# A decoder layer in fp32 on one core: the projection of cross attention three key blocks later

## The chip, the core and the metric

The kernel runs on one core of a Trainium2 chip. The metric is the device time of one execution in microseconds (us). TensorE (PE) does the matmuls, VectorE (DVE), ScalarE (ACT) and GpSimd (POOL) the rest, SyncE (SP) issues the transfers. Each engine works through its own queue in order and waits on semaphores.

## What is computed

A decoder layer on x of 2048 tokens by 256: causal self attention with 16 heads of 16, cross attention with 16 heads of 64 to a context of 1601 rows, then a small feed-forward product in fp8 values. What matters here is the cross attention:

```python
q = (query @ Wq + bq).reshape(b, sq, N_HEAD, KEY_DIM)
k = (key @ Wk + bk).reshape(b, key.shape[1], N_HEAD, KEY_DIM)
v = (value @ Wv + bv).reshape(b, value.shape[1], N_HEAD, VALUE_DIM)
scores = jnp.einsum('bqhd,bkhd->bhqk', q, k) / TEMP
attn = jax.nn.softmax(scores, axis=-1)
out = jnp.einsum('bhqk,bkhd->bqhd', attn, v).reshape(b, sq, N_HEAD * VALUE_DIM)
out = out @ Wo + bo + residual
```

## The kernel before

All work is laid out in one list of stages, which the class `Order` makes. Each engine's program walks through the same list and issues what it has to do for each stage, so a stage's place in the list sets its place in every queue.

Cross attention goes through 8 pairs of heads (`NP`, p = 0 to 7), and in each pair through 4 blocks of 512 queries (`NB`, b = 0 to 3). A block of queries meets 13 key blocks of up to 128 rows (`NS`, j = 0 to 12):

- `pair_scores` (TensorE L904, L912): scores of one key block into one of four PSUM buffers for each head; ScalarE takes the exponentials (L1079) into a ring of 11 weights buffers. GpSimd adds the exponentials up over the key blocks (L698, one addition for each head and key block from j = 1 on), for the softmax's divisor. In the last pair VectorE adds for one of the two heads.
- `pair_values` (L924): products with the values, summed over the key blocks in PSUM.
- `pair_finish` (ScalarE L1093): the products are copied to one of two buffers `o_pair`. The next block's products for j = 0 wait for that copy.
- `pair_sums` (TensorE L935, ScalarE L976): the sums over the rows of the added exponentials, copied to `pair_recip`.
- `pair_invert` (VectorE L1283): four reciprocals of 128 columns.
- `pair_divide` (GpSimd L1434): `o_pair` times the reciprocals.
- `pair_project` (TensorE L947): the projection with the output weights: four tiles of queries, into two of the three PSUM banks that the side work also uses. VectorE adds each bank to the residual (L1292). After the fourth block of a pair, SP loads the output weights of the pair after the next (L1457).

The score steps run in groups of two key blocks. After each group, `pair_values` of `Order` counts as many steps as key blocks are pending, and puts in the stages that have come due; only then it puts in the products of the group before. `after(n, ...)` makes a stage come due n steps on. With `SUMS_LAG` the sums follow the finish by 4 steps. From the sums, the reciprocals follow by 1 to 4 steps, the division by 5 and the projection by `PROJECT_LAG` = 8, so by 12 from the finish. As a block has 13 steps, the projection of a block stands after the scores of key block 12 of the next block, and ahead of the next block's products of 10 and 11.

Into this main work the side work is spread: the first sweep of the next pair (`pair_chunk`: scores for the maxima, TensorE L889, VectorE L1189; `pair_negate` and `pair_rows` for the shifts), and the next but one pair's projections of keys (L723, then ScalarE L1055 and L1064, VectorE L1252, GpSimd L1422) and queries (ScalarE L1058, VectorE L1239) and the value tiles (L877). This side work shares the three banks in turn. The projections of keys stand around the beginning of each pair. The last pair has no side work of this kind; its projections are followed by the tail of the layer (`tail`).

Of the kernel before, what the change touches and what calls it, by code (L numbers as in the profile page):

```python
# [21 lines left out]
NB, TB = T // BQ, BQ // P  # L22
# [3 lines left out]
FOLD_LAG, TURN_LAG, OUT_LAG = 2, 2, 2  # L26


SUMS_LAG, PROJECT_LAG = 4, TB + 4

SELF_RING, SELF_SCORES = 4, 3
CROSS_RING, NSCORES = 3, 4
# [9 lines left out]
NP = H // HP  # L42
# [76 lines left out]
class Order:  # L119
# [104 lines left out]
    def pair_sums(self, p, b):  # L224
        self.put("pair_sums", p, b, banks=1)
        for t in range(TB):
            self.after(t + 1, lambda t=t: self.put("pair_invert", p, b, t))
        self.after(TB + 1, lambda: self.put("pair_divide", p, b))
        self.after(PROJECT_LAG, lambda: self.pair_out(p, b))

    def pair_sweep2(self, p):
        batch = []
# [1402 lines left out]
```

## Time and profile before

| | us |
|---|---|
| median of 3 runs | 2157.15 |
| lowest, highest | 2141.8, 2167.85 |
| the profiled execution's own time | 2139.68 |
| its span, first to last instruction | 2137.7 |

The profile records one execution. PE is the matmul part of TensorE, PEld its weight loads. An instruction is named by its engine and by its line in the kernel (L947); each fp32 matmul of the kernel shows up as more than one record. PEclk is the clock that TensorE was granted as a share of 2.4 GHz; its two levels are 1.2 and 2.4 GHz. Cross attention lasts from about 727 us to the end, the last pair's own part from about 1956 us. The share of busy time of an engine over the span mixes stages, so the rows below are cut by stage. A row of waits names the engine and line that stood idle, and whose end came last before it went on.

### The profile page before, as it was taken

What the parts mean: (1) busy time and instruction counts of PE and PEld (TensorE: products, weight loads), DVE (VectorE), ACT (ScalarE), POOL (GpSimd) and SP (SyncE); (2) the same over time, 40 slices, a digit from 0 to 9 for tenths busy, and PEclk for the clock granted to TensorE, in tenths of its full rate; (3) what the DMA queues carried; (4) which work ended last, traced back from release to release, by engine and by line L of the source; (5) the groups of instructions that cost most, each with busy time, mean ns of one, the idle gap of its engine ahead of it and who ended that gap; (6) DMA issues with size and microseconds to landing.
All of it is one profiled execution on the core that took longest, in us unless ns stands there. A gap on an engine that the chain in (4) does not pass through costs nothing.

```text
span 2137.7 us, 29456 instructions
## 1 busy us (share of the span) xinstructions
PE 1862.8 (87%) x10650; PEld 949.8 (44%) x10650; DVE 1295.8 (61%) x2455; ACT 916.6 (43%) x1866; POOL 1036.1 (48%) x872
## 2 busy tenths in 40 slices
PE   6888999889998998898999899889889889989671
PEld 3544444434444544444445445445445445444331
DVE  4677766766712557746636545645654653667888
ACT  2235655555644343244343343344344434434331
POOL 1000000000000466558777777877876886886664
PEclk9669999998967899999999899999999999999875
DMA  5222201240011000000000000000000000000001
GB/s 106 29 33 32 32 8 25 32 88 1 1 30 40 19 1 1 1 10 12 1 1 12 1 1 12 1 1 12 2 1 3 1 1 3 1 10 21 0 21 39
DMA packets 28745, 34.46 MB, mean 16 GB/s; under 512 B 4099, under 2 KB 26948, under 8 KB 26948
## 3 DMA queue, kind: packets, MB, share of 16 engines
q1 hardware_dynamic: 28600, 32.59, 8.5%
q8 instruction: 85, 1.39, 0.3%
q14 instruction: 60, 0.48, 0.1%
HBM read 14.99 MB, written 4.19 MB: 9 GB/s over the span
## 4 chain that ended last, share of the span: by engine, by line
PE 47%; issue 26%; POOL 10%; DVE 8%; ACT 6%; SPq 2%; DMA 1%; POOLq 0%; ACTq 0%; DVEq 0%
PE psum L924 8%; POOL parts_room L698 7%; PE psum L809 7%; PE psum L904 6%; PE psum L784 5%; PE psum L757 4%; PE psum L947 4%; ACT weights_room L1007 3%; PE psum L889 3%; DVE maxima L1189 3%; PE psum L723 2%; POOL parts_room L1434 2%; PE psum L821 2%; ACT weights_room L1079 1%; PE psum L793 1%
## 5 line engine op out<-in xcount | busy, mean ns | idle before, releaser
L1189 DVE TENSOR_REDUCE maxima<-psum 128x1 f32<-128x400 f32 (+5 forms) x1664 | 864.1, 579 | 351.5 <-PE psum L889 192.4
L698 POOL TENSOR_TENSOR parts_room<-parts_room,weights_room 128x512 f32<-128x512 f32 (+1 forms) x606 | 761.2, 1284 | 133.1 <-ACT weights_room L1079 128.1
L1079 ACT ACTIVATE weights_room<-psum 128x512 f32<-128x512 f32 (+1 forms) x757 | 402.2, 601 | 568.8 <-PE psum L904 387.3
L1007 ACT ACTIVATE weights_room<-psum 128x512 f32<-128x512 f32 (+3 forms) x640 | 297.8, 535 | 248.2 <-PE psum L784 133.8
L1396 POOL TENSOR_SCALAR rstd<-meanvar 128x2 f32<-128x2 f32 (+1 forms) x24 | 8.0, 333 | 708.6 <-DVE meanvar L1139 708.6
L904 PE MATMUL psum<-stack_room,dk_hi 64*128 64x512 f32 (+1 forms) x1408 | 269.4, 410 | 18.7 <-ACT weights_room L1079 18.7
L889 PE MATMUL psum<-k_later,stack_room 64*128 64x400 f32 (+1 forms) x896 | 245.5, 404 | 33.1 <-DVE maxima L1189 32.0
L784 PE MATMUL psum<-stack_room,stack_room 51*128 51x512 f32 (+3 forms) x640 | 201.6, 452 | 45.9 <-ACT weights_room L1007 44.5
L889 PEld LDWEIGHTS psum<-k_later,stack_room 64*128 64x128 f32 x896 | 129.5, 184 | 205.3 <-issue 103.2
L924 PE MATMUL psum<-weights_room,parts_room 128*64 128x512 f32 (+1 forms) x754 | 211.5, 627 | 0.0
L924 PE MATMUL psum<-weights_room,late_room 128*64 128x512 f32 (+1 forms) x760 | 208.9, 622 | 0.0
L757 PE MATMUL psum<-stack_room,stack_room 51*128 51x512 f32 (+3 forms) x640 | 166.0, 480 | 19.5 <-DVE maxima L1189 13.5
L809 PE MATMUL psum<-weights_room,v_self 128*32 128x512 f32 (+3 forms) x1280 | 178.7, 614 | 0.0
L904 PEld LDWEIGHTS psum<-stack_room,dk_hi 64*128 64x128 f32 (+1 forms) x1408 | 148.9, 182 | 57.4 <-ACT weights_room L1079 31.4
L904 PE MATMUL psum<-stack_room,dk_lo 64*128 64x512 f32 (+1 forms) x704 | 173.9, 393 | 0.0
L947 PE MATMUL psum<-parts_room,parts_room 128*128 128x256 f32 x256 | 98.9, 553 | 72.9 <-POOL parts_room L1434 72.9
L784 PEld LDWEIGHTS psum<-stack_room,stack_room 51*128 51x128 f32 x640 | 97.2, 204 | 130.6 <-ACT weights_room L1007 107.9
L698 POOL TENSOR_TENSOR parts_room<-weights_room,weights_room 128x512 f32<-128x512 f32 x49 | 61.8, 1276 | 184.7 <-ACT weights_room L1079 184.7
L757 PEld LDWEIGHTS psum<-stack_room,stack_room 51*128 51x128 f32 x640 | 72.9, 206 | 141.1 <-issue 115.8
L1292 DVE TENSOR_TENSOR stack_room<-psum,stack_room 128x512 f32<-128x512 f32 x64 | 43.8, 690 | 128.9 <-PE psum L947 128.5
L1283 DVE RECIPROCAL parts_room<-parts_room 128x128 f32<-128x128 f32 x128 | 112.5, 918 | 0.0
L947 PEld LDWEIGHTS psum<-parts_room,parts_room 128*128 128x128 f32 x256 | 67.3, 275 | 96.9 <-POOL parts_room L1434 84.3
(133 smaller groups left out, 1987.5 us busy)
## 6 DMA issues: line engine op xcount, KB each, us to landing
stack_room<-parts_room SPq DMA_DIRECT2D x96, 128.0 KB
x_block<-x_dram SPq DMA_DIRECT2D x8, 512.0 KB, 4.8
x_middle<-x_block SPq DMA_DIRECT2D x4, 512.0 KB, 3.1
x_block<-x_middle SPq DMA_DIRECT2D x4, 512.0 KB, 3.9
out_dram<-x_block SPq DMA_DIRECT2D x8, 256.0 KB, 2.1
parts_room<-ctx_dram SPq DMA_DIRECT2D x1, 1536.0 KB
stack_room<-shift_rows SPq DMA_DIRECT2D x64, 2.0 KB
parts_room<-wq_dram SPq DMA_DIRECT2D x8, 128.0 KB, 2.2
```

What stands on the lines that cost most here:

```text
L698: engine.tensor_tensor(sum_[:kw, :], old[:kw, :], weights[u % NP_WEIGHTS][:kw, :], ALU.add) \
L757: last = engine.matmul(slots[m][:, 0:k1 - k0], q_stack[p % NSTACK][r, i * P:(i + 1) * P], k_stack[p % NSTACK][r, k0:k1], start=True, stop= ...
L784: last = engine.matmul(self_scores[u % SELF_SCORES][:, 0:n], k_stack[p % NSTACK][r, j * P:(j + 1) * P], q_stack[p % NSTACK][r, q0:q0 + n], ...
L809: last = engine.matmul(products[c:c + COL, q0:BQ], v_self[:, j0 + n, h * VW:h * VW + COL], w_self[(s0 + n) % NW][:, m, 0:BQ - q0], start=j ...
L889: filled(use + n, engine.matmul(slot[:, 0:k1 - k0], q_hi[p % 2][r:r + DH2, i * P:(i + 1) * P], k_high(p)[r:r + DH2, k0:k1], start=True, st ...
L904: last = engine.matmul(pair_scores[u % NSCORES][:kw, :], k[r:r + DH2, at:at + kw], q[r:r + DH2, block(b)], start=first and n == 0, stop=no ...
L924: engine.matmul(products[r:r + DH2, :], v_pair[p % 2][:kw, j, r:r + DH2], weights[u % NP_WEIGHTS][:kw, :], start=j == 0, stop=j == NS - 1) \
L947: last = engine.matmul(slot[:, t * D:(t + 1) * D], o_pair[n_block % 2][:, i * P:(i + 1) * P], wo2[p % 2], start=True, stop=True)
L1007: engine.activation(w_self[s % NW][:, m, 0:n], self_scores[(HP * s + m) % SELF_SCORES][:, 0:n], ACT.Exp, scale=SELF_SCALE).then_inc(exp_do ...
L1079: engine.activation(weights[u % NP_WEIGHTS][:kw, :], pair_scores[u % NSCORES][:kw, :], ACT.Exp, scale=CROSS_SCALE).then_inc(pair_exp, 1)
L1189: engine.tensor_reduce(maxima[:, p % 2, i // TB, n, i % TB, ch:ch + 1], bank_of(use + n)[:, 0:real - k0], AX.X, ALU.max) \
L1283: engine.reciprocal(pair_recip[:, cols], pair_recip[:, cols]).then_inc(inverted, 1)
```

## The change

The projection's lag counts 11 steps from the sums in place of 8, which is 15 from the finish, except in the last pair, where it stays at 8. Nothing else in the kernel differs.

```diff
-SUMS_LAG, PROJECT_LAG = 4, TB + 4
+SUMS_LAG, PROJECT_LAG, LAST_PROJECT_LAG = 4, TB + 7, TB + 4
...
         self.after(TB + 1, lambda: self.put("pair_divide", p, b))
-        self.after(PROJECT_LAG, lambda: self.pair_out(p, b))
+        self.after(PROJECT_LAG if p < NP - 1 else LAST_PROJECT_LAG, lambda: self.pair_out(p, b))
```

`TB` is 4. `pair_out` puts in the stage `pair_project`, the load of output weights after a fourth block, and in the last pair the tail.

## Rows read from the trace of the kernel before

**Rows 1.** The page's first part: busy time of each engine and its share of the span.

```profile
span 2137.7 us, 29456 instructions
...
PE 1862.8 (87%) x10650; PEld 949.8 (44%) x10650; DVE 1295.8 (61%) x2455; ACT 916.6 (43%) x1866; POOL 1036.1 (48%) x872
```

**Rows 2.** Table of stretches by projection: length, busy per engine (count), PEclk, DMA share, GB/s.

```profile
827.03:979.75 152.72, 139.94 (x721) 73.29 (x721) 95.49 (x181) 54.11 (x106) 96.19 (x80) 0.99 0.03 7
979.75:1142.51 162.76, 147.63 (x800) 77.42 (x800) 91.36 (x169) 68.16 (x133) 126.78 (x105) 0.98 0.02 5
1142.51:1313.16 170.65, 155.45 (x801) 81.15 (x801) 91.34 (x169) 68.18 (x133) 126.80 (x105) 0.92 0.02 4
1313.16:1481.08 167.92, 152.74 (x801) 80.37 (x801) 91.36 (x169) 68.17 (x133) 126.75 (x105) 0.94 0.02 5
1481.08:1643.97 162.89, 147.67 (x800) 77.07 (x801) 91.34 (x169) 68.17 (x133) 126.88 (x105) 0.98 0.01 2
1643.97:1808.31 164.34, 149.15 (x801) 78.74 (x801) 91.36 (x169) 68.17 (x133) 126.85 (x105) 0.97 0.01 2
1808.31:1955.68 147.37, 133.16 (x702) 68.03 (x702) 96.46 (x163) 60.41 (x117) 112.61 (x90) 0.91 0.04 12
```

**Rows 3.** Waits of cross attention, 727 to 1956 us: engine, line, releaser: total, times, longest.

```profile
POOL parts_room L698 <- ACT weights_room L1079: 281.5, 88, 25.3
...
DVE stack_room L1292 <- PE psum L947: 128.5, 50, 7.5
...
PE psum L947 <- POOL parts_room L1434: 70.7, 28, 3.8
...
PE psum L889 <- DVE maxima L1189: 36.3, 69, 0.8
```

**Rows 4.** Timeline of one stall, 1168 to 1186 us: start, duration, engine, line, work, idle before.

```profile
1172.46 2.20 ACT L1079 ACTIVATE weights_room<-psum 128x512 f32<-128x512 f32 x4 [2.25 <-PE psum L904]
...
1173.46 6.17 POOL L698 TENSOR_TENSOR parts_room<-parts_room,weights_room 128x512 f32<-128x512 f32 x5
...
1176.53 0.40 PE L904 MATMUL psum<-stack_room,dk_lo 64*65 64x512 f32 x2
...
1179.60 1.25 POOL L1434 TENSOR_TENSOR parts_room<-parts_room,parts_room 128x512 f32<-128x512 f32 x1
...
1180.91 3.78 PE L947 MATMUL psum<-parts_room,parts_room 128*128 128x256 f32 x8 [3.58 <-POOL parts_room L1434]
1183.02 0.69 DVE L1292 TENSOR_TENSOR stack_room<-psum,stack_room 128x512 f32<-128x512 f32 x1 [4.75 <-PE psum L947]
```

**Rows 5.** TensorE's timeline at five projections, between 975 and 1225 us.

```profile
979.75 1.99 PE L947 MATMUL psum<-parts_room,parts_room 128*128 128x256 f32 x8 [1.84 <-POOL parts_room L1434]
...
1015.22 3.62 PE L947 MATMUL psum<-parts_room,parts_room 128*128 128x256 f32 x8 [3.55 <-POOL parts_room L1434]
...
1054.28 1.99 PE L947 MATMUL psum<-parts_room,parts_room 128*128 128x256 f32 x8 [1.58 <-POOL parts_room L1434]
...
1089.58 2.90 PE L947 MATMUL psum<-parts_room,parts_room 128*128 128x256 f32 x8 [3.76 <-POOL parts_room L1434]
...
1220.85 3.78 PE L947 MATMUL psum<-parts_room,parts_room 128*128 128x256 f32 x8 [1.58 <-POOL parts_room L1434]
```

**Rows 6.** TensorE's timeline from a projection to the second pair of next products, 1952 to 1970 us.

```profile
1955.68 2.00 PE L947 MATMUL psum<-parts_room,parts_room 128*128 128x256 f32 x8 [2.18 <-POOL parts_room L1434]
1957.61 1.94 PE L924 MATMUL psum<-weights_room,late_room 128*64 128x512 f32 x8
...
1962.52 0.73 PE L904 MATMUL psum<-stack_room,dk_hi 64*128 64x512 f32 x4
...
1964.11 1.94 PE L924 MATMUL psum<-weights_room,late_room 128*64 128x512 f32 x8
```

**Rows 7.** Timeline around key projections, 1095 to 1125 us, where the third block's projection will stand.

```profile
1102.01 2.38 PE L723 MATMUL psum<-parts_room,parts_room 128*128 128x512 f32 x8
...
1105.33 1.00 DVE L1252 SCALAR_TENSOR_TENSOR parts_room<-psum,parts_room,parts_room 128x512 f32<-128x512 f32 x2 [2.28 <-ACT k_later L1055]
...
1105.90 1.98 PE L723 MATMUL psum<-norm_room,parts_room 128*128 128x512 f32 x4
...
1109.75 0.75 DVE L1239 SCALAR_TENSOR_TENSOR stack_room<-psum,parts_room,stack_room 128x512 fp32r<-128x512 f32 x1 [3.42 <-ACT stack_room L1058]
```

**Rows 8.** One line of the source, the reciprocals on VectorE, whole span: its head.

```profile
L1283 DVE RECIPROCAL parts_room<-parts_room x128: 887/937/947, 809.4 to 2098.4; 128x128 f32<-128x128 f32 x128
```

## The prediction

> **What bounds the kernel now.** I read the page's first part, then the stretches, then the waits, then a stall in its timeline. TensorE is busy for 87% of the span, the next engine for 61% [rows 1]. The change touches cross attention's first seven pairs, so the stretches are cut from one projection of a block to the same one a pair later [rows 2]: 162.76 to 170.65 us a whole pair (the last row is a shorter one), TensorE busy for 147.6 to 155.5 of it, GpSimd 126.8, VectorE 91.4, ScalarE 68.2. TensorE is the bound, and lacks some 15.2 us of being busy throughout in each pair.
>
> The waits say what most of that is [rows 3]. From 727 to 1956 us TensorE stood before the projection (L947) for GpSimd's division (L1434) 70.7 us in 28 waits: once for each of the four blocks of the seven pairs. Its wait for VectorE's maxima is next, 36.3 us in 69 pieces of at most 0.8. VectorE stood 128.5 us for the projection, since its addition (L1292) comes next in its queue; that is the same stall seen behind TensorE, not a second cost.
>
> The timeline shows why the division is late [rows 4]. It comes in GpSimd's queue behind the additions of key blocks 10 and 11. ScalarE makes their exponentials from 1172.46 to 1174.66, GpSimd does five additions in 6.17 us (1.234 each), then the division at 1179.60, to 1180.85. TensorE began the last matmuls of key block 12 at 1176.53 and was through 0.8 us later; it starts the projection at 1180.91. In a steady pair the four stalls are 1.8, 3.6, 1.6 and 3.8 us [rows 5].
>
> A second cost comes with them. Eight matmuls of the projection take 1.99 us at 979.75 and at 1054.28, and 3.78 us at 1180.91 and 1220.85 [rows 4, 5]. The granted clock falls from 2.4 to 1.2 GHz at the stalls: the pair with PEclk 0.98 lasts 162.89 us, the one with 0.92 170.65 [rows 2], with the same instructions.
>
> **The change part by part.** No instruction is added or removed; one step moves. It goes three key blocks later. Counted on TensorE's queue it passes the products of key blocks 10 and 11, the scores of key blocks 0 and 1 of the next block, the products of key block 12, the scores of 2 and 3, and the pieces of side work that lie between. It lands right ahead of the products of 0 and 1. The sums, the reciprocals and the division stay where they are. On ScalarE it has no instruction; on VectorE its two additions move past the maxima or key steps in between. GpSimd's queue doesn't have it. On SP, the load of the output weights (L1457, six times) moves with it; no transfer of shifts lies between the old place and the new, and these weights are wanted two pairs later. Buffers hold: the sums of two blocks alternate, and the eviction that needs the projected buffer again comes 26 key blocks after the first, against 15 for the projection.
>
> *Stall.* What TensorE has to do between the old place and the new is from the end of a projection to the second group of eight products. It is shortest where there is no side work: 1957.68 to 1964.11, 6.4 us [rows 6]; with side work it is more. The stall ahead of it is 2.2 us there, and no stall is over 3.8 [rows 3, 6]. So even the shortest way after the longest stall leaves the division ready with 2.6 us in hand, and the 70.7 us go. I take all of it; the lower bound is what follows if GpSimd falls further behind, below.
>
> *GpSimd's pace*, since it loses the pause that TensorE's stalls gave it. A block costs it 24 additions of 1.234 and a division of 1.25, 30.9 us [rows 4]. TensorE's shortest interval is from 979.75 to 1015.22, 35.47 us, less its stall of 3.55: 31.9; the third is 1089.58 - 1054.28 = 35.30, less 3.76: 31.5 [rows 5]. The other two of the pair are 39.06 and 52.93. GpSimd has 0.6 us to spare in the tight ones and 5 or more in the others. It keeps up, and does not build a queue from block to block.
>
> *Clock.* The share of a pair at 1.2 GHz is twice what PEclk lacks: 27.3 us of 170.65 and 6.5 of 162.89. The pairs differ by 7.76 us for 20.8 us more at the lower level: 0.37 us lost for each us. Less than a half, since part of such a stretch is the stall itself. Over the seven rows [rows 2] the time at the lower level is 3.1 + 6.5 + 27.3 + 20.2 + 6.5 + 9.9 + 26.5 = 100 us, times 0.37 is 37 us. The bounds are nothing (it falls anyway) and 50 us (one half of 100). I take 37, since every slow group of the projections' rows follows a wait, and TensorE has hardly any idle time left when these waits are gone.
>
> *The new place.* Two of three banks are taken at once there. In the third block of a pair it stands behind projections of keys, whose banks VectorE frees late. There the four blocks of keys are projected by 1104.4, VectorE's last key step ends at 1106.3, and TensorE finishes the first query projection at 1107.9 [rows 7]; so the banks are free when the projection comes. Behind it the next query projection needs a bank that is read at 1110.5, while TensorE has the projection (2.0) and products (1.9) to do first: nothing to wait for. I take 0; the bound is the 3.42 us that VectorE waited there for ScalarE, in one block of four: seven times 3.42, 24 us.
>
> *Sum.* 70.7 + 37 = 108 us off the profiled execution: span 2137.7 - 108 = 2030; its own time was 2139.68, 2.0 above its span, so 2032. The median of the runs, 2157.15, is 17.5 us above that execution. If this comes from more time at the lower clock at the stalls, the change takes it away too, and I take 2032 for the median; if it sits elsewhere, the time is near 2049.
>
> **The rivals.**
> 1. *GpSimd paces.* There is no addition for key block 0, so GpSimd may stand for one key block in each short block (31.7 / 13 = 2.4 us), which makes its block 33.3 where TensorE's is 31.7: 1.6 us in 14 blocks, 22 us, with half of the clock's gain lost, 18. Time 2072. For it: 30.9 against 31.5 is close. Against: GpSimd waited for ScalarE 281.5 us in cross attention [rows 3], so it has room, and a delay of its division is harmless until it passes the slack above.
> 2. *The clock stays as it is.* Only the stalls go: 2139.7 - 70.7 = 2069. For it: 36.3 us of short waits on maxima stay [rows 3]. Against: 979.75 and 1054.28 have stalls of 1.8 and 1.6 with no slow matmul, and between the stalls the rows show full speed. The Trainium skill, TensorE: Matmul & The Clock Gate, in the section on psum-queue depth-cycling, describes a kernel whose matmul groups run through PSUM banks with so many small idle moments that the clock oscillates. By it this ring of three banks would keep it oscillating, and the sum would be without its clock term; this trace has 0.99 in the first stretch, where VectorE reads banks most densely (181 instructions in 152.7 us against 169 in 162.8 [rows 2]).
> 3. *The gain is given back at once*: the stalls only absorb another engine's lateness, and TensorE waits as long at the next maxima or scores. 2140 to 2157. For it: VectorE and GpSimd work on or catch up meanwhile. Against: outside of the stalls TensorE is busy nearly all the time, and no engine is busy for more than 126.8 of the 148 us that a pair would take.
> 4. *Slower.* VectorE is late at the new place: the bank ring of three is held by its queue, four reciprocals of 0.918 [rows 8] and two additions of 0.69 [rows 4], 5.1 us, and TensorE waits for a bank behind each of 28 projections, its clock as low as now. That adds 143 us where 71 are saved: 2140 + 72 = 2212. It takes the whole gain of the stalls from 71 / 28 = 2.5 us a block, and is slower by over 1% of the median (2179) from (71 + 39) / 28 = 3.9. Against: the reciprocals are due three to six key blocks after the new place, and had been done long before the old one; VectorE is busy for 91 us of 165.
>
> **How the numbers follow.** The forecast (2010 to 2055) has 62%, rival 1 12%, rival 2 10%, rival 3 8%, rival 4 5%; 3% for a time under 2010. Predicted 2032. The low end is 2032 less the 13 us of the clock's upper bound and some lateness of the maxima that goes too, 2010; the high end takes in rivals 1 and 2 and the 24 us of bank waits beside part of the median's distance: 2085. A measurement of this kernel can tell about 1% from no change. Faster by over 1%: 62 + 12 + 10 + 3 = 87%. Within 1%: 8%. Slower: 5%.
>
> **What would show it.** In the profile after, no wait of L947 on L1434 in pairs 0 to 6 (the one of the last pair's first block stays, about 2.2 us). Pairs of 148 to 151 us between like projections, with TensorE busy for all but some 4 us, and eight projection matmuls in 1.99 us. PEclk 0.98 or more from 830 us to the last pair. GpSimd's busy time per pair stays 126.8. The last pair stays as long as it is. I would be wrong if L947 waited for a bank, if L1434 still ended after the place reached, if ScalarE waited for L698, or if TensorE showed 1.2 GHz in the middle of a block with no idle time before it.

## The result: 5.7% faster, and the stages that gave it

The changed kernel takes 2025.67 us in the median of 4 runs (2021.61 to 2040.59) against 2149.48 us before (2138.02 to 2167.85). The ratio is 0.943, with an interval of 0.934 to 0.952. The profiled execution has a span of 2026.2 us where the kernel before has 2137.7, 111.5 us less. The prediction had 2030 for the span and 2032 for the time. A ratio, here and below, compares only those executions that lie within 1.5% of the fastest of the same kernel, so it is not always the quotient of the medians.

The page after differs in few places: TensorE is busy 1815.9 us (90%) in place of 1862.8 (87%), with the same 10650 matmuls; VectorE (1297.4) and GpSimd (1041.1) do what they did. First the table of stretches of the kernel after; columns as in [rows 2]. The first row ends where the first scores of cross attention begin, the second at the sums (L935) of the first pair's fourth block. The three rows in the middle run from the fourth block's projection of a pair to that of the next. The last two are cut at the sums of fourth blocks again.

```profile
0.00:732.00 732.00, 640.84 (x4269) 318.48 (x4269) 435.03 (x899) 363.23 (x787) 26.92 (x40) 0.87 0.21 34
732.00:949.80 217.80, 204.56 (x1004) 105.59 (x1004) 141.10 (x274) 83.43 (x163) 138.60 (x115) 0.97 0.02 5
981.72:1130.62 148.90, 143.89 (x801) 75.80 (x801) 91.07 (x170) 68.23 (x135) 127.16 (x105) 1.00 0.02 5
1130.62:1279.52 148.90, 143.86 (x800) 75.89 (x801) 91.08 (x170) 68.21 (x135) 127.22 (x105) 1.00 0.02 5
1577.43:1726.39 148.96, 143.95 (x800) 76.01 (x801) 91.07 (x170) 68.21 (x135) 127.21 (x105) 1.00 0.01 2
1694.50:1830.20 135.70, 130.66 (x771) 70.34 (x770) 95.56 (x168) 59.69 (x116) 119.81 (x96) 1.00 0.04 13
1830.20:1973.80 143.60, 110.35 (x570) 51.47 (x568) 124.25 (x177) 60.12 (x117) 97.33 (x77) 0.87 0.02 8
```

And four stretches of the kernel before, with the cuts of the first two and the last two of these:

```profile
0.00:735.00 735.00, 644.35 (x4269) 319.67 (x4269) 435.39 (x899) 362.78 (x787) 26.88 (x40) 0.87 0.21 34
735.00:954.00 219.00, 202.80 (x1004) 102.49 (x1003) 141.03 (x274) 83.14 (x163) 138.33 (x115) 0.99 0.02 5
1782.60:1939.50 156.90, 141.73 (x769) 75.68 (x768) 95.44 (x174) 59.71 (x116) 118.90 (x96) 0.91 0.03 9
1939.50:2085.40 145.90, 111.18 (x570) 51.48 (x568) 121.10 (x171) 60.09 (x118) 95.54 (x77) 0.87 0.03 10
```

What the reader is to see: a whole pair lasts 148.9 to 149.0 us, every one, where [rows 2] had 162.8 to 170.7. TensorE is busy for 143.9 of that, so it lacks 5.0 us where it lacked 15.2; PEclk is 1.00 where it went down to 0.92. Up to the first scores the two differ by 3 us (735.0 against 732.0), which is no effect of the change, as its queues are the same there. So cross attention gave 108.5 of the 111.5 us: 1402.7 from first scores to the end before, 1294.2 after. The last pair, whose own order is as it was, takes 198.2 us before (145.9 and the 52.3 behind it) and 196.0 after (143.6 and 52.4); the difference is about the stall of the pair before it, 2.2 us, that fell into it.

The waits of cross attention after, from 727 to 1900 us, which takes in the first 50 us of the last pair's own part (columns as in [rows 3]):

```profile
POOL parts_room L698 <- ACT weights_room L1079: 194.3, 102, 26.1
...
PE psum L889 <- DVE maxima L1189: 37.1, 71, 0.8
...
DVE stack_room L1292 <- PE psum L947: 11.6, 37, 0.7
...
PE psum L947 <- POOL parts_room L1434: 2.5, 1, 2.5
```

The 28 waits for the division are gone. The one that is left, of 2.5 us, is the last pair's own first block; its like before (2.2 us) lies behind the window of [rows 3]. VectorE's wait for the projection went with them, 128.5 to 11.6 us. The maxima are as they were (36.3 before, 37.1 after): nothing was handed on to the next wait. GpSimd stands for the exponentials for 194 us where it stood for 281 [rows 3]: it has less idle time, as the same work stands in a shorter span.

The timeline at the same projection as in [rows 4], block 0 of the third pair, after the change:

```profile
1156.34 1.34 POOL L1434 TENSOR_TENSOR parts_room<-parts_room,parts_room 128x512 f32<-128x512 f32 x1
...
1162.40 0.52 PE L889 MATMUL psum<-k_later,stack_room 64*128 64x402 f32 x2
...
1162.85 1.99 PE L947 MATMUL psum<-parts_room,parts_room 128*128 128x256 f32 x8
1164.02 0.69 DVE L1292 TENSOR_TENSOR stack_room<-psum,stack_room 128x512 f32<-128x512 f32 x1 [0.15 <-PE psum L947]
```

The division ends at 1157.68, the projection begins at 1162.85, without idle time ahead of it and at full speed, 1.99 us for the eight matmuls. Here the division is 5.2 us ahead; in the other blocks of a steady pair 7.2, 10.8 and 6.3.

### The profile page after: what moved, and what is told of

Its sections match the earlier page's. It is cut to its first block, busy times and chain, and to the rows that moved or that the text cites. A ratio compares the mean times of both kernels' runs of the same rounds, so it can differ in the third digit from the quotient of the medians.

```text
span 2026.2 us, 29464 instructions
## 1 busy us (share of the span) xinstructions
PE 1815.9 (90%) x10650; PEld 931.0 (46%) x10650; DVE 1297.4 (64%) x2455; ACT 917.6 (45%) x1866; POOL 1041.1 (51%) x872
## 4 chain that ended last, share of the span: by engine, by line
PE 74%; DVE 15%; ACT 5%; issue 2%; SPq 2%; DMA 1%; POOL 1%; ACTq 0%; POOLq 0%; DVEq 0%
PE psum L924 16%; PE psum L904 14%; PE psum L889 8%; PE psum L809 7%; DVE maxima L1189 7%; PE psum L723 6%; PE psum L784 5%; PE psum L757 4%; ACT weights_room L1007 4%; PE psum L947 3%; PE psum L877 3%; DVE parts_room L1283 2%; PE psum L821 2%; PE psum L935 1%; DVE parts_room L698 1%
## 5 line engine op out<-in xcount | busy, mean ns | idle before, releaser
L698 POOL TENSOR_TENSOR parts_room<-parts_room,weights_room 128x512 f32<-128x512 f32 (+1 forms) x606 | 764.6, 1293 | 164.0 <-ACT weights_room L1079 158.3
L924 PE MATMUL psum<-weights_room,late_room 128*64 128x512 f32 (+1 forms) x760 | 204.4, 609 | 0.0
L924 PE MATMUL psum<-weights_room,parts_room 128*64 128x512 f32 (+1 forms) x754 | 202.7, 605 | 0.0
L757 PE MATMUL psum<-stack_room,stack_room 51*128 51x512 f32 (+3 forms) x640 | 165.6, 480 | 19.7 <-DVE maxima L1189 13.6
L904 PEld LDWEIGHTS psum<-stack_room,dk_lo 64*128 64x128 f32 (+1 forms) x704 | 98.4, 183 | 10.1
L924 PEld LDWEIGHTS psum<-weights_room,late_room 128*64 128x64 f32 (+1 forms) x760 | 51.4, 138 | 86.3 <-issue 83.3
L698 POOL TENSOR_TENSOR parts_room<-weights_room,weights_room 128x512 f32<-128x512 f32 x49 | 63.5, 1312 | 52.3 <-ACT weights_room L1079 52.3
L924 PEld LDWEIGHTS psum<-weights_room,parts_room 128*64 128x64 f32 (+1 forms) x754 | 50.8, 136 | 82.2 <-issue 78.8
```

The costliest lines, as they stand in the source:

```text
L698: engine.tensor_tensor(sum_[:kw, :], old[:kw, :], weights[u % NP_WEIGHTS][:kw, :], ALU.add) \
L757: last = engine.matmul(slots[m][:, 0:k1 - k0], q_stack[p % NSTACK][r, i * P:(i + 1) * P], k_stack[p % NSTACK][r, k0:k1], start=True, stop= ...
L904: last = engine.matmul(pair_scores[u % NSCORES][:kw, :], k[r:r + DH2, at:at + kw], q[r:r + DH2, block(b)], start=first and n == 0, stop=no ...
L924: engine.matmul(products[r:r + DH2, :], v_pair[p % 2][:kw, j, r:r + DH2], weights[u % NP_WEIGHTS][:kw, :], start=j == 0, stop=j == NS - 1) \
```

## Experiments

All are compared with the kernel before on the same chip. As the part of the program ahead of cross attention, which none of them touches, takes 722.0 to 736.2 us in their traces, a pair's length in the trace says more than the time. What the stretches show is one execution of each kernel.

### The clock's share alone

The stall is kept and filled: TensorE multiplies into the bank that the projection will overwrite.

```diff
+FILL = (6, 2, 6, 3)
...
-                pe.wait_ge(divided, n_block + 1)
                 pe.wait_ge(wo_pair_in[p % 2], 16 * (p // 2 + 1))
+                slot = take_bank(use)
+                for _ in range(FILL[b] if p < NP - 1 else 0):
+                    engine.matmul(slot[:, 0:D], ident[:, :], wo2[p % 2], start=True, stop=True)
+                pe.wait_ge(divided, n_block + 1)
```

> The kernel before, with matmuls that nobody reads put ahead of the projection's wait for the division in pairs 0 to 6: 6, 2, 6 and 3 of them (128x256, about 0.5 us each at full speed) for blocks 0 to 3, written to the bank that the projection overwrites. TensorE works instead of standing, so the stalls' time stays and only the clock may change. If 37 us of the gain are the clock's, as predicted: about 2140 - 37 = 2103 (ratio to before 0.98), PEclk 0.98 or more in the steady pairs, and pairs of some 160 us. If the clock fell for another reason, or its fall cost nothing: no change, 2140 and PEclk of 0.92 to 0.98 as before. If the clock were most of the gain: near 2050.

Measured: 2100.02 us (2094.08 to 2137.18), ratio 0.974 (0.968 to 0.981). A pair of its table of stretches, and its timeline at the third pair's block 0. In this kernel L945 is the filling, L951 the projection and L1438 the division:

```profile
1109.70:1269.30 159.60, 152.60 (x837) 81.96 (x836) 91.39 (x169) 68.17 (x133) 126.92 (x105) 1.00 0.02 5
...
1167.43 2.83 PE L945 MATMUL psum<-parts_room,ident 128*128 128x256 f32 x12
1169.59 1.25 POOL L1438 TENSOR_TENSOR parts_room<-parts_room,parts_room 128x512 f32<-128x512 f32 x1
...
1170.90 1.78 PE L951 MATMUL psum<-parts_room,parts_room 128*128 128x256 f32 x7 [0.64 <-POOL parts_room L1438]
```

All five steady pairs are 159.5 or 159.6 us. The projection still waits for the division, 0.64 us behind the filling that ends at 1170.26, but now takes its full speed. So the same order with the same lateness, without the fall of the clock, is 159.6, and 148.9 without the stalls: 10.7 us a pair are the stalls, which is the 10.8 read in [rows 4, 5]. What the clock cost is the rest: 3 us in the pairs that had 0.98, 11 us in the one with 0.92. From the first pair's last sums to the last pair's last sums (seven stretches), 1131.4 us before became 1089.7 here and 1024.0 in the changed kernel: 41.7 for the clock, 65.7 for the stalls. The expectation had 37 and some 2103 us.

### The cause: the division's place in GpSimd's queue

The projection stays at its old place; the division comes one step earlier, ahead of the additions of key blocks 10 and 11.

```diff
-        self.after(TB + 1, lambda: self.put("pair_divide", p, b))
+        self.after(TB, lambda: self.put("pair_divide", p, b))
```

> The kernel before, with the projection where it was and the division one step earlier, so that it stands ahead of the additions of key blocks 10 and 11 in GpSimd's queue. If the cause is that the division was behind four additions, no stall of L947 on L1434 is left and the gain is the whole of the change's: about 2030, ratio 0.945. If the later place of the projection itself brought something (the banks, the queue of VectorE), less than that: the stalls go, but pairs stay above 149 us. If GpSimd now stands for VectorE's reciprocals and falls behind with its additions, a part comes back as a wait for L1434 or L698: 2060 to 2100.

Measured: 2036.86 us (2025.81 to 2042.83), ratio 0.945 (0.939 to 0.951). Two of its stretches, a steady pair and the one before the last sums, and its timeline at two projections:

```profile
1095.70:1244.60 148.90, 144.25 (x801) 75.83 (x800) 91.41 (x169) 68.16 (x133) 126.88 (x105) 1.00 0.02 5
1827.90:1977.70 149.80, 110.95 (x571) 51.85 (x570) 125.43 (x173) 60.05 (x117) 94.17 (x76) 0.86 0.03 11
...
1148.78 1.27 POOL L1434 TENSOR_TENSOR parts_room<-parts_room,parts_room 128x512 f32<-128x512 f32 x1
...
1150.01 3.74 POOL L698 TENSOR_TENSOR parts_room<-parts_room,weights_room 128x512 f32<-128x512 f32 x3
...
1151.58 1.75 PE L947 MATMUL psum<-parts_room,parts_room 128*128 128x256 f32 x7
...
1843.22 1.76 DVE L1283 RECIPROCAL parts_room<-parts_room 128x128 f32<-128x128 f32 x2
...
1845.12 1.51 POOL L1434 TENSOR_TENSOR parts_room<-parts_room,parts_room 128x512 f32<-128x512 f32 x1 [6.18 <-DVE parts_room L1283]
...
1846.69 1.65 PE L947 MATMUL psum<-parts_room,parts_room 128*128 128x256 f32 x3 [4.85 <-POOL parts_room L1434]
```

The pair is 148.9 us, the same as with the change, though only GpSimd's queue was touched. So the stall was the division's lateness behind four additions; the later place of the projection brings nothing beyond that. The division ends 1.5 us ahead of the projection here. But where VectorE adds too, in the last pair, the same order stalls by 4.85 us: there the division at the head waits for VectorE's reciprocals (1843.22 to 1844.98), and the stretch is 149.8 us against 143.6 with the later projection. The two ways are alike in the steady pairs. At the end the later projection is some 6 us shorter in these two traces, which the times (0.945 and 0.943, with intervals that overlap) can't tell.

### Half of the blocks

The change for blocks 0 and 2 alone.

```diff
-        self.after(PROJECT_LAG if p < NP - 1 else LAST_PROJECT_LAG, lambda: self.pair_out(p, b))
+        self.after(PROJECT_LAG if p < NP - 1 and b in (0, 2) else LAST_PROJECT_LAG, lambda: self.pair_out(p, b))
```

> The change for blocks 0 and 2 only, where the stalls were 3.6 and 3.8 us in a steady pair; blocks 1 and 3, with 1.6 and 1.8, keep the old place. Stalls of 46 us go and 24.4 stay. If short stalls do not bring the clock down by themselves, the whole clock term (37) goes too: 2140 - 46 - 37 = 2057, ratio 0.961, and eight projection matmuls take 1.99 us in all blocks. If each stall brings it down on its own, half of that term: 2076, ratio 0.97, with 3.8 us projections in blocks 1 and 3.

Measured: 2065.05 us (2054.7 to 2077.38), ratio 0.959 (0.952 to 0.967). Two neighbouring pairs, and the projections of blocks 1 and 3 in the third pair:

```profile
948.60:1103.60 155.00, 147.15 (x803) 77.72 (x802) 91.11 (x169) 68.17 (x133) 126.87 (x105) 0.98 0.02 5
1103.60:1255.50 151.90, 144.05 (x801) 75.89 (x800) 91.12 (x169) 68.19 (x133) 126.91 (x105) 1.00 0.02 5
...
1198.57 1.78 PE L947 MATMUL psum<-parts_room,parts_room 128*128 128x256 f32 x7 [1.58 <-POOL parts_room L1434]
...
1281.23 2.07 PE L947 MATMUL psum<-parts_room,parts_room 128*128 128x256 f32 x4 [1.86 <-POOL parts_room L1434]
```

The pairs go 155.0, 151.9, 155.1, 151.9, 153.6. With 148.9 + 1.6 + 1.8 = 152.3 for a pair with its two short stalls and a full clock, 151.9 is that, and 155 is that with slow matmuls. In the rows, a stall of 1.58 us is followed by fast matmuls, one of 1.86 by slow ones (2.07 us for the four that the line holds). Over the six pairs from 950 us on, both outcomes occur for both lengths (1.58: slow in 2 of 6, 1.86: slow in 4 of 6), and the granted clock is 1.00 in the 3 us ahead of each. So a short stall alone can bring the clock down, but not each time. The seven stretches take 1061.1 us: 1024.0, 22.8 of stalls, and 14.3 more. Of these, 2.5 us are a wait of TensorE for ScalarE's exponentials at 1851.92, which neither the kernel before nor the changed one has; the rest, under 12 us, is mainly the clock, against its 41.7 before. The ratio is that of the first expectation, but its mechanism is not quite: it had no slow matmuls left.

### The exception for the last pair

The change without its exception.

```diff
-SUMS_LAG, PROJECT_LAG, LAST_PROJECT_LAG = 4, TB + 7, TB + 4
+SUMS_LAG, PROJECT_LAG, LAST_PROJECT_LAG = 4, TB + 7, TB + 7
```

> The change without its exception: the last pair's projections too come three key blocks later, and the tail of each block, which starts with its projection, with them. Pairs 0 to 6 stay as in the changed kernel (149 us). In the last pair one wait for the division goes (2.5 us), and the tails of blocks 0 to 2 start some 5 us later, where VectorE is the busier engine. If VectorE has no room there, the end comes later by about 5 us: near 2031. If it has, it is the same or 2 us less: 2024 to 2028. If the exception were what made the change good, clearly slower than 2040.

Measured: 2025.51 us (2015.85 to 2038.51), ratio 0.941 (0.934 to 0.948). Its last two stretches:

```profile
1823.40:1959.50 136.10, 107.31 (x564) 48.63 (x562) 120.53 (x168) 59.71 (x116) 95.08 (x74) 0.87 0.03 8
1959.50:2014.00 54.50, 12.00 (x52) 6.34 (x52) 46.58 (x103) 10.49 (x20) 23.55 (x28) 0.53 0.12 39
```

136.1 and 54.5 us where the changed kernel has 143.6 and 52.4: 5.4 us less at the end. But from the first scores to the end it has 2014.0 - 723.1 = 1290.9 us against 1294.2. Both were run once more.

> The changed kernel without its exception once more. In the first run its pair before the end was 136.1 us where the changed kernel has 143.6, and the stretch behind the last sums 54.4 against 52.4: 5.5 us less. If that holds, its ratio to the kernel before is 0.2 to 0.3% lower than that of the changed kernel, near 2021.

> The changed kernel once more, for comparison with its form without the exception on the same chip: near 2026, ratio 0.943.

Measured: 2020.19 us (2014.7 to 2048.64), ratio 0.945 (0.939 to 0.952) without the exception, and 2021.28 us (2014.31 to 2028.87), ratio 0.945 (0.940 to 0.950) with it. From first scores to the end it is 1289.6 without and 1290.3 with. The times show no difference: 0.2 to 0.3% is less than they can tell. The sums from the first scores on don't tell either, as they hold the first pair's stretch, which varies by 4 us (215.2 to 219.6) with falls of the clock. The stretches behind it do show one. The last two stretches with the exception are 143.6 + 52.4 = 196.0 and, the second time, 142.1 + 52.4 = 194.5; without it 136.1 + 54.5 = 190.6 and 137.0 + 54.1 = 191.1. From the first pair's last sums to the end it is 1076.4 and 1075.1 us with the exception, 1071.3 and 1071.7 without, while the steady pairs are 148.9 to 149.1 in all four traces. So the exception does not make the change; it costs some 3 to 5 us, close to the 5.5 read from the first trace. The wait of 2.5 us for the division is part of it; the rest was not traced.

### How much room GpSimd has

The changed kernel with more multiplications on GpSimd ahead of each division, into a buffer that is not read then; two of them, then four.

```diff
+                for _ in range(2 if at[0] < NP - 1 else 0):
+                    chain.on(engine.tensor_tensor(added[n_block % 2][:, 0, :], o_pair[n_block % 2], pair_recip,
+                                                  ALU.mult))
+                    after_last()
                 engine.tensor_tensor(o_pair[n_block % 2], o_pair[n_block % 2], pair_recip, ALU.mult) \
```

> The changed kernel with two more multiplications on GpSimd ahead of each division in pairs 0 to 6, into a buffer that nobody reads then. That is 2.5 us a block later for the division and everything behind it. In the changed kernel the division is done 5.2, 7.2, 10.8 and 6.3 us ahead of the projection in the blocks of a steady pair, and 2.7 and 0.8 us in the two projections that fall into the last pair. If there is room, only the last one stalls, by some 2 us: pairs of 149 us, time 2026 to 2032 where the changed kernel has 2026. If GpSimd paces already (rival 1), each block pays: 28 times 2.5, near 2095.

Measured: 2030.4 us (2023.87 to 2050.98), ratio 0.951 (0.942 to 0.959). A steady pair:

```profile
1099.00:1248.10 149.10, 144.11 (x803) 76.09 (x802) 91.11 (x169) 68.18 (x133) 137.16 (x113) 1.00 0.02 5
```

GpSimd does 137 us of work in 149, 10 more than before, and the pair's length doesn't move. In block 0 the division still ends 2.1 us ahead of the projection. Only the last moved projection stalls, by 4.7 us rather than the 2 I had expected: there the three multiplications take 5.5 us (1850.50 to 1855.97), where the division alone took 1.5.

> The same with four such multiplications: 4.9 us a block, GpSimd's work 35.8 us where TensorE's shortest interval between projections is 32.2, and 146.5 of 149 us over a pair. If the reserve is what the trace of the changed kernel shows, GpSimd falls behind in the short blocks by more than the 5.2 us: the waits for the division come back, 1 to 4 us in one or two blocks of each pair, and the slow clock with them: 3 to 8 us a pair, time 2050 to 2085. If the reserve is larger: as the changed kernel.

Measured: 2073.07 us (2070.84 to 2092.46), ratio 0.972 (0.962 to 0.981). A steady pair and its timeline at the third pair's block 0, where L1435 is the added work and L1438 the division:

```profile
1105.40:1259.30 153.90, 145.68 (x801) 76.53 (x800) 91.12 (x169) 68.23 (x133) 146.96 (x121) 0.99 0.02 5
...
1166.09 5.34 POOL L1435 TENSOR_TENSOR parts_room<-parts_room,parts_room 128x512 f32<-128x512 f32 x4
...
1171.51 1.26 POOL L1438 TENSOR_TENSOR parts_room<-parts_room,parts_room 128x512 f32<-128x512 f32 x1
...
1172.82 2.60 PE L947 MATMUL psum<-parts_room,parts_room 128*128 128x256 f32 x7 [3.22 <-POOL parts_room L1438]
```

With 147 us of 154 GpSimd now paces in the one place where the interval is shortest: block 0 stalls by 3.2 us in every pair, the matmuls behind it are slow, and the pair is some 5 us longer. The other three blocks have no wait for the division. So rival 1 exists, but only above the load that the kernel has: 127 us a pair is free, 137 still is, 147 isn't.

## Why the prediction was right

**The bound and the stall.** Both held: 70.7 us of waits in 28 pieces went, one of 2.5 us in the last pair stayed (2.2 forecast). The pairs were to be 148 to 151 us and are 148.9. TensorE was to lack some 4 us in each and lacks 5.0.

**The sum.** 108 us forecast; 108.5 in cross attention, 111.5 over the span, the rest being the 3 us before it. Its two terms are now measured apart. The clock's was forecast 37 and is 41.7 over seven stretches. The slope of 0.37 us for a microsecond at the lower level was a little low: by PEclk the first six of these stretches held 99 us at that level before (the seventh takes 145.9 us with the filling too), and 41.7 over 99 is 0.42. The stalls' was 70.7, of which 3.8 lie ahead of those stretches; 66.9 against 65.7 measured. In the stretch with the first pair's stalls (3.8 us) the profiled execution gained only 1.2 (219.0 to 217.8), as its clock fell three times there (0.97, where the kernel before fell once and had 0.99); in the second profile of the changed kernel, with one fall, that stretch is 215.2, which is the 3.8. So the sum hits closer than its terms: a clock term that was 4.7 too low and stalls that gave back 3.8 less (65.7 and 1.2 for 70.7) nearly cancel, and that part of the closeness is luck.

**GpSimd's pace.** I had worked out that it keeps up with 30.9 us of work a block against intervals of 31.5 and more. The intervals after are 32.2, 36.2, 37.8 and 42.7 us, as the projection now stands in other places of the side work, and it does keep up. The 31.5 was taken from the old places and belongs to no interval after. With two multiplications a block costs it 33.4 us, more than the shortest 32.2, and still nothing stalls in the steady pairs; the division's lead in block 0 goes from 5.2 to 2.1. That the limit was near, as rival 1 said, is shown too, with its distance.

**The slack** was the weak step. I said 2.6 us at least between division and projection. In the steady pairs it is 5.2 and more. In the last one that was moved it is 0.8:

```profile
1848.25 1.54 POOL L1434 TENSOR_TENSOR parts_room<-parts_room,parts_room 128x512 f32<-128x512 f32 x1 [3.69 <-DVE parts_room L1283]
...
1850.61 1.99 PE L947 MATMUL psum<-parts_room,parts_room 128*128 128x256 f32 x8
...
1872.50 3.26 PE L947 MATMUL psum<-parts_room,parts_room 128*128 128x256 f32 x8 [2.53 <-POOL parts_room L1434]
```

These are the last moved projection (1850.61) and the first that isn't (1872.50, with its stall). GpSimd had stood 3.69 us for VectorE's reciprocals, which I had counted as ready: in the last pair VectorE also adds exponentials, and they come in its queue among these additions. They were done 13.6 us behind the sums in the kernel before (1939.52 to 1953.08) and 18.0 here (1830.16 to 1848.11). I had read the old stall's length there as GpSimd's lateness alone. It was within the room, and cost nothing; with two multiplications more it was not, and gave the 4.7 us above.

**The new place** cost next to nothing, where I took nothing. L947 does wait for a bank, which I had named as a sign of being wrong: 2.9 us in six pieces, for ScalarE's copy of the shifts, in the second block of a pair. The third block's projection, among the keys, has no wait. Another sign, ScalarE waiting for L698, showed once, for 1.9 us at the beginning of the last pair, behind VectorE's additions. Neither is of a size that bears on the sum.

**Rival 2**, the clock stays, fell: 1.00 in all steady pairs, with the same short waits on maxima. The Trainium skill, TensorE: Matmul & The Clock Gate, on psum-queue depth-cycling, tells of a kernel whose small idle moments between matmul groups keep the clock oscillating. In the steady pairs of this one such moments, of at most 0.8 us, do not; the measurement decides for this kernel. But in the first pair they are all that stands ahead of the clock's three falls. Groups of scores of the same size ahead of one and behind it:

```profile
910.46 0.62 PE L904 MATMUL psum<-stack_room,dk_hi 64*128 64x512 f32 x4
...
914.83 1.40 PE L889 MATMUL psum<-k_later,stack_room 64*128 64x400 f32 x3 [0.67 <-DVE maxima L1189]
...
917.71 1.55 PE L904 MATMUL psum<-stack_room,dk_hi 64*128 64x512 f32 x4
```

The granted clock is 1.00 from 911 to 915 us and 0.73 from 915 to 920; the other two falls follow waits for maxima of 0.47 us (786.80) and 0.48 us (830.77). TensorE waits for maxima 11.0 us in this stretch of 217.8, and 4.3 in a steady pair of 148.9. The two falls more than in the second profile of this kernel go with 2.6 us (217.8 and 215.2). What tells the first pair from the others was not tested. **Rival 3** fell with the waits after, where nothing took the place of the one removed. **Rival 4**, a bank held by VectorE, fell with the 11.6 us that VectorE waits for the projection and with no bank wait of L947 behind VectorE.

**The median.** I took the predicted 2032 for the median rather than 2049, betting that the distance of the median before from its profiled execution came from the clock at the stalls. The median came out at 2025.67, and at 2021.28 in the second series, while the kernel before stayed near 2150. The kernel with the filled stalls points the same way: by the times it gains 2.6%, some 55 us, where the traces have 41.7 for the clock. But its interval, 0.968 to 0.981, is 41 to 70 us, so where those 10 to 17 us lie is not shown, and the bet was not more than that.

## What to carry to other kernels

When the bounding engine waits for a result at the head of its queue, look in the queue of the engine that makes it for what stands ahead: the fix may be on either side, a later consumer or an earlier producer, and both gave the same 149 us a pair. Price the stall with its aftermath: here 65.7 us of waits carried 41.7 us of slow matmuls. Before counting on it, compare the producer's work per block with the consumer's shortest interval after the change, and look at the stages where a third engine has more to do, since the slack goes there first.

## What the runs showed of the hardware

A stall of 1.6 to 1.9 us on TensorE had the matmuls behind it run at 1.2 GHz in some cases and not in others, in one and the same execution. The last pair's stall of 2.5 us in the changed kernel did so in one execution (3.26 us for the eight matmuls) and not in the other (1.99). All stalls of 3.2 us and more did. Waits of 0.5 to 0.7 us for maxima did not in the steady pairs, and stood ahead of three falls in the first pair.

Filling the stall with matmuls whose result nobody reads, with gaps of 0.4 to 1.0 us left, kept 2.4 GHz in every steady pair (PEclk 1.00) and was worth 41.7 us in the traces, 2.6% by the times (1.9 to 3.2%).
